# Scan preparation in another order: B's later split, the first decays and dx's turn

## What is computed

```python
x = jax.nn.silu(conv)                        # 64 images, 37 tokens, 128 channels
delta = jax.nn.softplus(x @ W_delta + b_delta)
Bm = x @ W_B + b_B                           # 64 states
Cm = x @ W_C + b_C
A = -jnp.exp(A_log)
dA = jnp.exp(delta[..., None] * A)
dBx = delta[..., None] * Bm[:, :, None, :] * x[..., None]

def step(h, inputs):
    dA_t, dBx_t, C_t = inputs
    h = dA_t * h + dBx_t
    y_t = jnp.einsum('bdn,bn->bd', h, C_t)
    return (h, y_t)
```

## Time and profile before

| | us |
|---|---|
| median of 3 runs (1146.85 to 1149.83) | 1148.17 |
| the profiled execution, its own time | 1147.44 |
| its span in the profile | 1145.6 |
| DVE busy in the span | 666.4 |
| PE busy in the span | 926.5 |

### The profile page before, as it was taken

One profiled execution on the slowest core, in us unless ns is written; L12 is line 12 of the kernel. 1 busy time (PEld: TensorE's weight loads), 2 busy tenths in 40 slices (PEclk: granted clock), 3 DMA queues, 4 the chain that ended last, 5 costly groups with the idle time before them and its releaser, 6 DMA issues.

```text
span 1145.6 us, 17578 instructions
## 1 busy us (share of the span) xinstructions
PE 926.5 (81%) x5861; PEld 587.7 (51%) x5862; DVE 666.4 (58%) x1161; ACT 509.1 (44%) x1028; POOL 305.4 (27%) x361
## 2 busy tenths in 40 slices
PE   8997262577777777669899999989999997459896
PEld 6774230233332333235677777757666674336564
DVE  1533834588888898875455445437777783313332
ACT  1227371577778877514322222234445432223332
POOL 5912921133333331000000000035444330422222
PEclk9998656798899988989999999979999997579999
DMA  6292369522222121352521211000000000522230
GB/s 235 93 328 85 106 174 247 129 49 50 53 49 52 35 53 30 119 216 110 229 86 53 75 42 42 0 1 1 1 1 0 0 1 10 221 97 82 79 95 25
DMA packets 92706, 96.07 MB, mean 84 GB/s; under 512 B 64350, under 2 KB 78687, under 8 KB 90976
## 3 DMA queue, kind: packets, MB, share of 16 engines
q1 hardware_dynamic: 89904, 87.91, 25.2%
q0 software_dynamic: 2736, 7.30, 1.7%
HBM read 61.57 MB, written 34.59 MB: 84 GB/s over the span
## 4 chain that ended last, share of the span: by engine, by line
PE 63%; ACT 12%; DVE 10%; issue 6%; SPq 4%; DMA 3%; another core or an unknown queue 0%; POOL 0%; ACTq 0%; DVEq 0%; POOLq 0%
PE ps L554 8%; PE ps L612 8%; PE ps L1173 6%; ACT mem L1601 5%; PE ps L1055 4%; PE ps L1457 4%; PE ps L1473 4%; PE ps L1370 3%; PE ps L1304 3%; PE ps L1133 3%; SPq L814 2%; ACT mem L1626 2%; PE ps L1326 2%; PE ps L1140 2%; DVE mem L1904 2%
## 5 line engine op out<-in xcount | busy, mean ns | idle before, releaser
L1012 POOL TENSOR_TENSOR mem<-mem,sm 128x296 f32<-128x296 f32 x128 | 87.1, 714 | 352.6 <-ACT mem L1691 312.5
L1601 ACT ACTIVATE mem<-ps 128x512 f32<-128x512 f32 x288 | 153.9, 634 | 42.8 <-DMA factor_rows<-mem 30.2
L990 POOL TENSOR_SCALAR mem<-mem,sm 128x16 f32<-128x16 f32 x148 | 102.9, 718 | 203.3 <-PE ps L1173 203.3
L1133 PE MATMUL ps<-mem 64*128 64x128 bf16 x1140 | 92.0, 230 | 53.5 <-ACT mem L1601 44.2
L1133 PEld LDWEIGHTS ps<-mem 64*128 64x128 bf16 x1140 | 55.9, 99 | 121.6 <-ACT mem L1601 103.7
L1912 DVE TENSOR_TENSOR ps<-mem 128x512 f32<-128x512 f32 x144 | 93.5, 695 | 42.0 <-ACT mem L1626 41.5
L554 PE MATMUL ps<-mem 128*128 (+1 forms) x384 | 108.6, 413 | 0.6 <-DVE mem L527 0.6
L1626 ACT ACTIVATE mem<-ps 128x512 f32<-128x512 f32 x148 | 82.3, 607 | 54.0 <-PE ps L1140 53.8
L1173 PE MATMUL ps<-mem 128*32 128x512 f32 x592 | 87.3, 663 | 22.1 <-issue 13.6
L1904 DVE TENSOR_TENSOR mem<-mem 128x1024 f32<-128x1024 f32 x72 | 87.7, 1218 | 25.0 <-ACT mem L1601 25.0
L1140 PE MATMUL ps<-mem 64*128 64x512 bf16 x296 | 76.7, 421 | 31.6 <-DVE ps L1912 21.6
(11 more groups left out here) (230 smaller groups left out, 1605.6 us busy)
## 6 DMA issues: line engine op xcount, KB each, us to landing
mem<-gates SPq DMA_DIRECT2D x7, 1184.0 KB, 6.0
mem<-in_w SPq DMA_DIRECT2D x2, 4096.0 KB, 17.7
slots<-mem SPq DMA_DIRECT2D x1, 6682.0 KB, 23.7
mem<-slots SPq DMA_DIRECT2D x26, 257.0 KB, 2.6
mem<-in_patches SPq DMA_DIRECT2D x7, 864.0 KB, 4.5
mem<-factor_rows SPq DMA_DIRECT2D x296, 16.0 KB, 1.8
mem<-factor_rows SPq DMA_DIRECT2D x37, 128.0 KB, 2.3
mem<-delta_rows SPq DMA_DIRECT2D x9, 512.0 KB, 4.5
```

The source lines that it names most:

```text
L990: nc.gpsimd.tensor_scalar(c_win4[:, t % SLOTS * 2 + r, :, w0:w0 + 8].rearrange("p j (x i) -> p j x i", i=2)[:, :, :, i], c_all[:, r * 16:r ...
L1133: mm = nc.tensor.matmul(ps[:, ring_bank(at_), e * BT:(e + 1) * BT], a_stat[64 * r:64 * r + 64, g, e, :], delta_in[b % 2][64 * r:64 * r + 6 ...
L1601: nc.scalar.activation(decay_slots[b % 2][:, :, 4 * k:4 * k + 4], ps[:, ring_bank(at_), :].rearrange("p (e t) -> p t e", e=4), ACT.Exp).th ...
```

## The change

Nothing is computed otherwise; the work is placed otherwise in time, on engines and in memory.

```diff
-        b_rest = at(0, THALF * P).rearrange("p (t n) -> p t n", t=THALF)
-        dx_rest = at(2432, THALF * P).rearrange("p (t n) -> p t n", t=THALF)
-        delta_rest = at(14336, T).rearrange("p (i l q) -> p i l q", i=2, l=L)
+        b_rest = [at(0, 4 * P).rearrange("p (t n) -> p t n", t=4),
+                  home(9984, (THALF - 4) * P).rearrange("p (t n) -> p t n", t=THALF - 4)]
+        dx_rest = [home(15584 + n * 512, 512).rearrange("p (t n) -> p t n", t=4) for n in range(2)]
+        delta_rest = [at(14336, 2 * 9 * PAIRS).rearrange("p (i l q) -> p i l q", i=2, q=PAIRS),
+                      at(28160, 2 * (L - 9) * PAIRS).rearrange("p (i l q) -> p i l q", i=2, q=PAIRS)]
...
-        DX_BANKS = (0, 1, 2, 3, 7)
+        DX_BANKS = (3, 7, 4, 5, 6)
...
-            sp.wait_ge(piece_cut, 8)
+            sp.wait_ge(piece_cut, 7)
             store_dx(0)
...
-            sp.wait_ge(piece_cut, 6)
+            sp.wait_ge(piece_cut, 9)
             store_delta(1)
             sp.wait_ge(b_split, 8)
             store_b(1)
-            sp.wait_ge(piece_cut, 16)
+            sp.wait_ge(piece_cut, 25)
             store_dx(1)
...
+            split_b(0)
             pool.wait_ge(c_copied, NCH + 2)
             pool.wait_ge(zeros_set, 4)
             for t in range(L):
+                if t == 4:
+                    pool.wait_ge(piece_cut, 25)
+                    split_b(1)
...
             pe.wait_ge(dx_ready, NQ)
+            pe.wait_ge(b_biased, 8)
...
                 if k < DECAY_BANKS:
-                    pe.wait_ge(piece_cut, 6 + 2 * k + 1)
...
-            pe.wait_ge(piece_cut, 15)
-            pe.wait_ge(b_biased, 6)
+            pe.wait_ge(piece_cut, 25)
...
                 act.wait_ge(made, at_ + 1)
+                if yb == 0:
+                    act.wait_ge(b_split, 8)
...
-            act.wait_ge(piece_cut, 16)
-            act.wait_ge(b_split, 8)
+            act.wait_ge(dx_ps, 5)
+            act.wait_ge(b_split, 4)
             for k in range(QUADS):
                 exp_quad(0, k)
...
+            multiply_x(0)
+            multiply_x(1)
+            cut_first(0, 0)
+            multiply_x(2)
+            multiply_x(3)
+            dve.wait_ge(piece_copied, 3)
+            cut_last(0)
+            cut_first(1, 3)
+            ts, got, rest = turned(0)
...
+            l0, l1, _, _ = RANGES[1]
+            dve.wait_ge(piece_cut, 5)
+            nc.vector.tensor_copy(delta_part[:, 1, :, l0:l1, :], delta_rest[1]).then_inc(piece_cut, 1)
+            dve.wait_ge(piece_cut, 8)
+            cut_last(1)
+            for k in range(1, 5):
+                ts, got, rest = turned(k)
+                dve.wait_ge(dx_ps, k + 1)
+                nc.vector.tensor_copy(dx_part[:, 0, ts, :], got).then_inc(piece_cut, 1)
+                dve.wait_ge(piece_cut, 4 * k + 6)
+                nc.vector.tensor_tensor(rest, got, dx_part[:, 0, ts, :], ALU.subtract).then_inc(piece_cut, 1)
+                dve.wait_ge(piece_cut, 4 * k + 7)
+                nc.vector.tensor_copy(dx_part[:, 1, ts, :], rest).then_inc(piece_cut, 1)
+                dve.wait_ge(piece_cut, 4 * k + 8)
+                nc.vector.tensor_tensor(dx_part[:, 2, ts, :], rest, dx_part[:, 1, ts, :],
                                         ALU.subtract).then_inc(piece_cut, 1)
```

More of the change, by code:

```diff
@@ L1578, in _ @@
             act.wait_ge(h_out, 16)
[L1579 to L1584, removed]
-                                     ACT.Copy).then_inc(piece_copied, 1)
[L1586 to L1590, removed]
-                                     ACT.Copy).then_inc(piece_copied, 1)
-                act.wait_ge(piece_cut, 6 + 2 * k + 1)
-                nc.scalar.activation(dx_part[:, 1, ts, :], dx_rest[:, ts, :], ACT.Copy).then_inc(piece_copied, 1)
+            (r0, r1, _, _), (late0, late1, _, _) = RANGES
+            for i in range(2):
+                nc.scalar.activation(delta_part[:, 0, i, r0:r1, :], delta4[:, i, r0:r1, :],
+                                     ACT.Copy).then_inc(piece_copied, 1)
+            act.wait_ge(piece_cut, 2)
+            nc.scalar.activation(delta_part[:, 1, :, r0:r1, :], delta_rest[0], ACT.Copy).then_inc(piece_copied, 1)
+            for i in range(2):
+                nc.scalar.activation(delta_part[:, 0, i, late0:late1, :], delta4[:, i, late0:late1, :],
+                                     ACT.Copy).then_inc(piece_copied, 1)
+            act.wait_ge(dx_ps, 1)
+            nc.scalar.activation(dx_part[:, 0, 0:4, :].rearrange("p t n -> p (t n)"), ps[:, DX_BANKS[0], :],
+                                 ACT.Copy).then_inc(piece_copied, 1)
+            act.wait_ge(piece_cut, 6)
+            nc.scalar.activation(dx_part[:, 1, 0:4, :], dx_rest[0], ACT.Copy).then_inc(piece_copied, 1)
             def exp_quad(b, k):
@@ L1867, in _, with multiply_x, cut_first @@
             dve.wait_ge(delta_ready, NQ)
-            for q in range(NQ):
+            delta4 = delta.rearrange("p (i q l) -> p i l q", i=2, q=PAIRS)
+            def multiply_x(q):
                 nc.vector.tensor_tensor(paired(dx, q * QI, QI), images(delta, q * QI, QI), paired(xs, q * QI, QI),
                                         ALU.mult).then_inc(dx_ready, 1)
-            delta4 = delta.rearrange("p (i q l) -> p i l q", i=2, q=PAIRS)
-            for r, (l0, l1, _, _) in enumerate(RANGES):
+            def cut_first(r, copied0):
+                l0, l1, _, _ = RANGES[r]
@@ L1880, in _, with cut_last, turned @@
[L1880 removed]
+            def cut_last(r):
+                l0, l1, _, _ = RANGES[r]
+                nc.vector.tensor_tensor(delta_part[:, 2, :, l0:l1, :], delta_rest[r],
                                         delta_part[:, 1, :, l0:l1, :], ALU.subtract).then_inc(piece_cut, 1)
[L1882 to L1890 removed]
+            def turned(k):
+                n = min(4, THALF - 4 * k)
+                return slice(4 * k, 4 * k + n), ps[:, DX_BANKS[k], 0:n * P].rearrange("p (t n) -> p t n", t=n), \
+                    dx_rest[k % 2][:, 0:n, :]
```

51 lines of the change are left out of this document (23 added, 28 removed).

## The result

| | us |
|---|---|
| before, median of 4 runs (1146.85 to 1149.83) | 1147.87 |
| after, median of 4 runs (1130.13 to 1134.89) | 1132.74 |
| ratio, with 95% interval | 0.9865 (0.9837 to 0.9893) |
| the profiled execution after, its own time / its span | 1134.89 / 1133.0 |

The change makes the kernel 15.5 us faster by the ratio (12.3 to 18.7). The forecast gain of 12.5 us lies in both intervals, near the lower end of the first; the forecast time, 1135.7 with a range from 1133.0, missed the first median by 0.3 us at its lower end.

A forecast was written before the change was run, and what follows sets the result against it. The landing of the last factor store, for which ACT waits, bounds this part; the stores' 45.7 us move as a whole. Started 12.5 us earlier, they land at 198.2 instead of 210.7: 1148.2 - 12.5 = 1135.7 us, range 1133 to 1140.

The forecast's parts named there:

- the last step of the sum: From the profiled execution, 1134.9 us, to the median of runs, set 0.73 us above it: 1135.7 us.
- transfers that overlap better: Case of transfers overlapping better than now, with DVE faster than thought, giving a time below 1133 us; chance 0.08.
- B's split out of DVE's way: DVE's softplus and dx no longer wait for POOL's later split; first delta store 11.15 us earlier.
- dx's first store: SyncE's queue: `store_dx(0)` issued at 131.8 instead of 145.77, directly behind `load_delta(0)`; its landing 12.5 us earlier (11.1 to 13.97).
- Range 1 ready in time: DVE's cuts end at 145.6 and POOL's split at 158.7, before SyncE wants B at 159.4, so nothing waits.
- the cover: Slack of B's later split: ending at 158.7, it costs nothing up to 162.0, thus 3.3 us.
- the first decays: ACT's exponentials of block 0 end at 151.6 instead of 169.3; worth nothing, since DVE waits for the last store anyway.
- The stores' own time: From `store_delta(1)` to the last landing 45.7 us without a gap, the transfers' own time, moving as a whole with its start.
- The windows: Rival: DVE waits for each of POOL's sixteen windows beside softplus and dx, losing 5.4 us; time 1141.1; chance 0.08.
- A late split: Rival: POOL's split, stretched beside the scan, ends at 168.7 and delays the stores by 6.7 us; time 1142.4; chance 0.08.
- POOL starves: Rival: the scan on DVE holds up POOL's split until 194.5, the kernel loses 20 us, time 1168; chance 0.03.
- nothing moves but copies: Rival: softplus and dx are slow by their access patterns, not by POOL; time within 3.4 us of before; chance 0.03.

The follow-up runs named there:

- split_only: The kernel before with only POOL's part of the change, B's later split moved behind sixteen windows and the last cut: 1136.28 us, ratio 0.9900 to before.
- split_early: The changed kernel, but POOL splits range 1 of B directly behind range 0, as before, and writes the windows after it: 1142.12 us, ratio 0.9967 to before.
- decays_late: The changed kernel, but ACT begins block 0's exponentials only when all pieces are cut and B is wholly split: 1131.73 us, ratio 0.9876 to before.
- halves_mixed: The changed kernel, but the stores of dx and B alternate between the two halves of 64 partitions: 1121.99 us, ratio 0.9785 to before.
- windows_aside: The changed kernel, but POOL writes the windows of steps 0 to 3 behind B's later split too: 1134.35 us, ratio 0.9896 to before.
- split_later: The changed kernel, but POOL begins B's later split only when ACT has copied step 0's state: 1145.45 us, ratio 0.9956 to before.

## Why the prediction missed, and where it held

**What failed is the last step of the sum, from the profiled execution to the median, and the lower end of the range around it.** The prediction took 12.5 us off the profiled execution of before and came to 1134.9; the profiled execution after was 1134.89. It then set the median 0.73 us above that, because the median of three runs had stood so before. After the change the median of four stood 2.15 us below, at 1132.74. For this the range left no room: its own terms, a shift of 13.97 and one us of DVE's, give 1148.2 - 14 - 1 = 1133.2 before any spread of runs, and the whole range began at 1133.0. The three runs shown spread by 3 us, and I took that for the spread. It is larger: before on one chip gave 1140.77 to 1150.14 in 17 runs, 9.4 us, and the changed kernel 1127.48 to 1135.23 in 6, 7.8 us. The code ahead of the changed stretch moves by 4 us and the code behind the scan by 6.6 us, as the traces show. Medians of before in the other sets lay between 1145.1 and 1149.1, so a median of a few runs moves by more than the 0.3 us by which the range was missed. The prediction gave a time below 1133 a chance of 0.08, but for transfers that overlap better; the stores took as long as before, 46.2 and 45.5 us against 45.7.

**The agreement of the profiled executions is in part luck.** The spans differ by 12.6 us. Of these 1.7 lie ahead of B's bias, where nothing was changed, 12.0 in the stretch, and behind it the changed kernel lost 1.1.

**The gain held.** The prediction said 12.5 us; the stretch says 12.0 and 12.9, the ratios 15.5 and 12.7. In the first two traces the 12.0 are 12.4 us by which `store_delta(1)` went earlier against the bias, less 0.5 by which the stores took longer.

**B's split out of DVE's way: right, and the larger part.** The first delta store moved against the bias by 23.6 - 12.15 = 11.5 us (135.47 - 111.86), said 11.15. split_only and split_early show 10 to 11 us for this part alone.

**dx's first store: right.** It went 0.04 us behind `load_delta(0)`'s issue. The unknown, what the closeness costs, lay between nothing and 2.85 us. Against the bias the store went 14.1 us earlier (33.9 before, 19.8 after) and the loads started 13.2 us earlier (40.4 before, 27.2 after), so 0.9 was lost, and I had taken 1.5. The third group of loads then issued in 4.56 us instead of 3.8, and `store_delta(1)` was 12.4 us earlier: two small errors that cancel.

**Range 1 ready in time: right, by more than said.** `piece_cut` 25 was at 140.8, which is 30.7 behind the bias, where 145.6 - 111.86 = 33.7 was said. Mis-sized were the copies on DVE within `mem`: 1.09 us for 1792 and 0.43 for 512, where I took 2.1 and 0.65 from a COPY out of PSUM. For the copy of 512 out of PSUM 0.65 was right, it took 0.68. The split took 11.45 us, not 13.1: the 2.33 and 4.22 us of the earlier trace rows had DVE beside them, and without it the CAST took 1.78 and the subtraction 3.82. Both errors lay under the cover and cost nothing. So did a slip in the sum for the first decays: 135.5 and 15.79 are 151.3, not 151.6.

**The first decays are worth nothing: right,** shown by decays_late.

**The stores' own time: right as a length, wrong as a limit.** It was 45.7 us in both traces of before, and 46.2 and 45.5 in those of the changed kernel. But "the transfers' own time" was the time of stores that use one half of the partitions each, in groups of three; halves_mixed took 10 us off it.

**The rivals.** The windows hold nothing up, shown by windows_aside: the exclusive lock of the prediction's rule does not show for instructions as small as these. A late split costs one for one behind 2 to 3 us of cover, shown by split_later, but in the changed kernel it ended at 152.35, 4.6 us ahead of SyncE's wait for it. That POOL starves did not show: in split_later it was DVE that lost most. That nothing moves but copies is out by split_only.

## What to carry to other kernels

Compare traces by a stretch between two named instructions around the change, since the spans of the same code differed by 4 us ahead of it and by 6.6 us behind it; and give a forecast of a single median the spread of many runs, not that of three. Where the chain of waits ends in transfers, bringing work forward on the engines is worth as much as it brings forward the first of those transfers (here within half a us, in the change, in split_early and in split_only), and moving other transfers about in the same queue can be worth nothing, since their issue is what fills it. Look at the rate of a long row of stores before taking its length for given: an alternating order of the same stores was worth almost as much as the whole change.

## What the runs showed of the hardware

Stores from one half of the partitions ran at about 200 to 220 GB/s in a row, delta's stores from all of them at 377, and stores of alternating halves at 318 on the mean, all in one queue and with the DMA engines' share at about 1.0 each time. Loads that issue in some 0.45 us on a queue with room took 1.7 us each (46.3 us for 27, most of 16 KB) when another engine issued them beside a full queue. A CAST from f32 to bf16 within `mem` on DVE took 1.09 us for 1792 elements, where the subtraction of as many took 2.03 and a CAST of 512 out of PSUM 0.68. And POOL's 128x16 instructions took 1.05 us each beside DVE's work without slowing its quarters, while its 128x1920 ones held DVE's products of two inputs in `mem` until they ended: 4.38 us for one of 0.76, and 3.7 for one of 1.2.
